# A running total of three propagation layers: its seven adds per layer move from VectorE to GpSimd

## The reference, cut to what matters

```
N_NODES = 18750; NNZ = 250000; LATENT = 64; MINI = 16; N_LAYERS = 3
def propagate(all_emb, rows, cols, vals):
    acc = all_emb
    x = all_emb
    for _ in range(N_LAYERS):
        x = segment_sum(vals[:, None] * x[cols], rows, num_segments=N_NODES)
        acc = acc + x
    return acc / (N_LAYERS + 1)
rating = sigmoid(users_emb @ items_emb.T + bias_user[users] + bias_item.T)
```

## Time and profile before

| what | us |
|---|---|
| median of 3 runs | 5368.86 |
| lowest and highest | 5368.59, 5371.43 |
| the profiled execution | 5364.2 |
| its span, first to last instruction | 5362.3 |
| VectorE busy | 4779.3 (89%) |
| TensorE matmul busy | 3360.9 (63%) |
| GpSimd busy | 2473.0 (46%) |
| ScalarE busy | 2466.3 (46%) |

### The profile page before, as it was taken

How to read it: one execution, slowest core, us unless ns; L and a number is a source line. 1 busy time by engine, 2 the same in 40 slices (tenths; PEclk the granted TensorE clock), 3 DMA queues, 4 the chain that set the end, 5 groups by cost and what they waited for, 6 DMA issues and landing times.

```text
span 5362.3 us, 195922 instructions
## 1 busy us (share of the span) xinstructions
PE 3360.9 (63%) x71235; PEld 2862.9 (53%) x71473; DVE 4779.3 (89%) x7551; ACT 2466.3 (46%) x4385; POOL 2473.0 (46%) x2179
## 2 busy tenths in 40 slices
PE   5600021111388888777688888867768888867767
PEld 4500011110377777666577777756657777766652
DVE  9989999999999999877899999967799999977778
ACT  0025555554466666500166666620046666640027
POOL 0038764433277777700067777720037777760000
PEclk9955555555699999999989999989989999989999
DMA  9960000300288877799978788889968877879999
GB/s 328 415 264 0 0 0 3 5 0 0 84 249 250 248 245 247 228 328 328 278 218 251 247 251 251 246 277 328 328 196 255 251 247 246 252 244 328 328 282 357
DMA packets 840271, 1191.20 MB, mean 222 GB/s; under 512 B 150791, under 2 KB 667582, under 8 KB 839824
## 3 DMA queue, kind: packets, MB, share of 16 engines
q1 hardware_dynamic: 716032, 816.66, 53.6%
q0 software_dynamic: 123872, 372.78, 18.2%
q10 hardware_dynamic: 304, 1.00, 0.1%
HBM read 638.35 MB, written 551.90 MB: 222 GB/s over the span
## 4 chain that ended last, share of the span: by engine, by line
DVE 27%; DMA 27%; issue 21%; POOL 10%; PE 7%; ACT 5%; SPq 1%; DVEq 1%; POOLq 0%; another core or an unknown queue 0%; ACTq 0%
DMA ring<-posts 15%; POOL posts L803 9%; DMA posts<-ring 8%; DVE store L1092 6%; PE psum L1543 4%; DVE total L889 3%; DVE ring L1313 3%; DVE store L1070 3%; ACT new L711 3%; DVE store L1071 2%; DMA out<-new 2%; DVE new L1285 2%; DVE ring L1337 2%; PE psum L1519 2%; DVE ring L1298 1%
## 5 line engine op out<-in xcount | busy, mean ns | idle before, releaser
L803 POOL DMA_INDIRECT posts<-ring x1884 | 1851.0, 982 | 1554.2 <-DVE ring L1298 962.3
L1519 PE MATMUL psum<-store,ring 128*128 x45216 | 2088.8, 197 | 485.0 <-DVE ring L1313 450.5
L1519 PEld LDWEIGHTS psum<-store,ring 128*128 128x128 bf16 x45216 | 1818.2, 100 | 755.7 <-issue 576.7
L711 ACT ACTIVATE new<-new 128x512 bf16<-128x512 uint8 x1884 | 1067.8, 614 | 0.0
L1313 DVE TENSOR_SCALAR ring<-ring,lane_f 128x1024 bf16<-128x1024 bf16 x1884 | 963.1, 553 | 10.7 <-DMA ring<-lanes_d 9.5
L1337 DVE TENSOR_TENSOR ring<-ring,wide_lane 128x1024 bf16<-128x1024 bf16 x948 | 613.3, 689 | 299.7 <-ACT ring L722 299.7
L1298 DVE TENSOR_TENSOR ring<-new 128x1024 bf16<-128x1024 bf16 x942 | 652.5, 693 | 92.4 <-ACT new L711 63.3
L709 ACT ACTIVATE ring<-new 128x512 bf16<-128x512 bf16 x942 | 585.8, 622 | 297.2 <-DVE new L1285 292.3
L767 POOL TENSOR_TENSOR ring<-store 128x1024 f32<-128x1024 f32 x157 | 369.6, 2354 | 662.7 <-DVE store L1010 306.4
L1285 DVE TENSOR_TENSOR new<-psum,vals_m 128x512 f32<-128x512 f32 x942 | 644.5, 684 | 6.9 <-PE psum L1519 4.9
L1429 PE MATMUL psum<-ident,store 128*128 128x128 f32 x224 | 51.6, 424 | 725.9 <-DVE store L1071 725.9
(11 more groups left out here) (232 smaller groups left out, 2728.0 us busy)
## 6 DMA issues: line engine op xcount, KB each, us to landing
ring<-lanes_d SPq DMA_DIRECT2D x471, 512.0 KB
ring<-posts SPq DMA_DIRECT2D x240, 772.0 KB, 6.7
store<-posts SPq DMA_DIRECT2D x234, 772.0 KB, 6.7
posts<-store SPq DMA_DIRECT2D x2, 30880.0 KB, 166.7
posts<-store SPq DMA_DIRECT2D x2, 30108.0 KB, 128.5
out<-new SPq DMA_DIRECT2D x96, 500.0 KB, 8.5
posts<-ring POOLq DMA_INDIRECT x1884
store<-L_rec_bias_item SPq DMA_DIRECT2D x1, 3125.0 KB, 14.6
```

What stands on the lines that cost most here:

```text
L711: last = nc.scalar.activation(digits[s][:, k, :], scaled_byte[s][k], ACT.Copy, scale=scale)
L803: pool.indirect_dma_start(out=posts[:, :], out_offset=bass.IndirectOffsetOnAxis(ap=dring[:, h, c:c + 1], axis=0), in_=msg[:, n, :], in_off ...
L1519: last = pe.matmul(psum[:, d % 4, (n % 2 * BLOCK + b) * F:(n % 2 * BLOCK + b + 1) * F], of, xflat[:, bass.ds(at_d[c] * F + (k * XT + x * F ...
```

## The change

GpSimd now runs the seven pieces of the running total at the head of each layer's program, ahead of its first scatter. In layer 0 it waits for the tables to be written (s_lanesd, s_decoded) and for x (s_x0), in the others for the last add of the layer before (s_add). VectorE's `take` and its seven calls are gone. The waits for s_taken stand as they were.

```
@@ gpsimd
             for layer in range(LAYERS):
                 done = layer * CHUNKS
+                if layer:
+                    pool.wait_ge(s_add, layer * ITERS + 2)
+                else:
+                    pool.wait_ge(s_lanesd, 64)
+                    pool.wait_ge(s_decoded, 1)
+                    pool.wait_ge(s_x0, 1)
+                for q in range(SPLITS):
+                    a, b = q * SPLIT, (q + 1) * SPLIT
+                    if layer == 0:
+                        nc.gpsimd.tensor_copy(total3[:, a:b, :], new3[:, a:b, :]).then_inc(s_taken, 1)
+                    else:
+                        nc.gpsimd.tensor_tensor(total3[:, a:b, :], total3[:, a:b, :], new3[:, a:b, :], ALU.add).then_inc(s_taken, 1)
+
                 def scatter(i, chunks):
@@ vector
-            def take(layer, q):
-                a, b = q * SPLIT, (q + 1) * SPLIT
-                if layer == 0:
-                    nc.vector.tensor_copy(total3[:, a:b, :], new3[:, a:b, :]).then_inc(s_taken, 1)
-                else:
-                    nc.vector.tensor_tensor(total3[:, a:b, :], total3[:, a:b, :], new3[:, a:b, :], ALU.add).then_inc(s_taken, 1)
-
@@ vector, send(i, first, pairs)
                         if not (first and d < 3):
                             low_parts(i, (d + 5) % 8, d - 3)
-                        if first and d < SPLITS:
-                            take(layer, d)
```

## The result

The changed kernel takes 5511.16 us in the median (3 runs, 5508.76 to 5518.41) against 5368.86: a ratio of 1.0264, interval 1.025 to 1.0278. It is slower, as forecast, but by 142 us and not by 31.5, far outside the range. Its profiled execution has a span of 5516.6, which is 154.3 above that of the kernel before.

What follows compares the result with a forecast made beforehand. VectorE was taken to bound the splits and first pairs. 24.6 us for layers 1 and 2 plus 6.9 for layer 0, gains deducted, made 31.5 on top of 5368.9: 5400.4 us, range 5376 to 5416.

Steps and rivals of the forecast that it cites:

- The split of layers 1 and 2: GpSimd's seven adds take turns with VectorE's 14 subtractions, making each of these splits 18.1 us longer.
- the first rival: In the splits, mixed-type subtractions don't exclude GpSimd; only the 13.7 us gain is left, 5355 us; chance 0.08.
- the second rival: GpSimd is kept out of the splits until the pairs begin, six adds delaying the first scatter; 5384 us; chance 0.08.
- the third: In the splits both engines share instead of excluding each other, at half the price; 5377 us; chance 0.06.
- Layer 0: GpSimd's seven copies, taken at 1.5 us each, make VectorE's chain ahead of the pairs 9.0 us later.
- the 0.9 won back: VectorE's own part in seven turns is 1.42 us in place of 1.55, 0.9 us less per layer.
- the lower bound of the earlier trace: Layer 0's copy at the memset's rate: 1.14 us for 1344 elements, VectorE's chain 6.5 us later.
- The gain in the first pairs: Pieces leaving VectorE bring pair 6 sooner: 2.1 us in layer 0, 5.8 each in layers 1 and 2, 13.7 in all.
- The stages are timed by each other, not by a clock, so an earlier start is kept: The first pairs' 13.7 us gain lasts to the end of each first half.
- If the split grows as foretold and the time still doesn't, the first half has a limit that I have not seen: Closing sign: longer splits without the foretold time would point to an unseen limit in the first half; no size given.

Runs made afterwards that it cites:

- x18: The changed kernel with one GpSimd add of one element behind layer 0's seven copies; 5377.51 us against 5344.68, ratio 1.0056.
- x8: The changed kernel with a one-element VectorE memset ahead of each pair's one-hot matrices; 5392.10 us, 43 above the kernel before.
- x5: The kernel before with one GpSimd copy of one element just before layer 0's first scatter; 5488.24 us, ratio 1.0212.
- x16: The kernel before with one GpSimd copy of one element and one add behind it, ahead of layer 0; 5342.68 us against 5342.72.
- x11: The kernel before with a one-element VectorE memset ahead of each pair's one-hot matrices; 5336.80 us, ratio 0.9986.

## Why the prediction was wrong, and where it was right

- **The split of layers 1 and 2: right.** Forecast 18.1 us each, measured 18.0. A turn of both engines is 4.29 us (2716.57 to 2725.16 is two), so GpSimd's own part is 2.87 beside VectorE's 1.42; the step had 2.9 and 1.42. Float32 and bfloat16 mixed exclude GpSimd as float32 alone does, which ends the first rival. The turn goes to and fro until the adds are done, 12 us before the one-hot matrices: not the second rival. All price and no sharing: not the third.
- **Layer 0: the copy was mis-sized, within its bounds.** Seven take 18.00 us in turns, 2.57 each; less VectorE's 1.42 that is 1.15 where the step took 1.5. 7 x 1.15 less the 0.9 won back is 7.1, and the split grew by 7.2 (forecast 9.0). It is the price of the memset, the lower bound of the earlier trace rows. The estimate from the Trainium skill's figure (GPSIMD Engine Reference, Elementwise — side-by-side cycle accounting) was 1.15 as well: the trace agrees.
- **The gain in the first pairs: right in size.** Forecast 2.1, 5.8 and 5.8. In the changed kernel it was 1.6, 5.4 and 4.8, and in x18, with scatters of the old length, 2.1, 6.4 and 6.3. The 25.6 us that the step took for pair 6 lie between the 25.0 and 26.8 of these. TensorE's granted clock in layer 1's first pairs (2758.2 to 2790) was 1.00, as the step had it, where it had been 0.61.
- **"The stages are timed by each other, not by a clock, so an earlier start is kept": the step that failed.** It asked only whether 13.7 us are kept, and took for granted that the pace of the other 307 pairs stays. They are timed by each other, and that makes them sensitive: a scatter 11 ns longer moved each one-hot matrix from just above to just below 91 ns behind a scatter. Two terms were put at nothing. Some 187 more scatters were held (201 against 14); at the 0.70 us of the rows above that is an estimate of 131 us. And 1884 scatters that are 11 ns longer are another 20. Of the 141 us that the scatters grew by from pair 6 on, that leaves 121 for the held turns, so the estimate is somewhat high; 19 us less between the scatters make it 122.
- **The order of GpSimd's instructions was in the text, and priced by its duration alone.** The views of before show the pace of the half, and no view shows that the kind of an earlier instruction matters. What could have been seen is the other link: the one-hot matrices of 1.09 us in place of 0.87 behind a scatter of 0.96, with starts 0.10 apart. That is a turn decided by little, in a loop of 942 rounds, and a line in the rivals with 100 us against it would have widened the range.
- **"If the split grows as foretold and the time still doesn't, the first half has a limit that I have not seen"** is what came true. With that limit taken away, x18 has the forecast's sum: 32.8 us measured (22 to 37 by its interval), 31.5 foretold. That the two are so close is partly luck: x18's splits and first pairs, read from its trace, add up to 43.2 - 14.8 = 28.4.

What stays open: why a copy as the last computing instruction ahead of layer 0's scatters makes each of the 1884, and the gathers behind the layers (most often 952 ns in place of 944), about 10 ns longer, and not those ahead of it, and why a copy ahead of layer 1 does nothing. The runs show the rule for this program, not what inside GpSimd is behind it. And the step from 11 ns to the edge is argued from the rows; that the lost turns are most of the cost is shown by x8, and that the 11 ns by themselves are some 20 us of it is an estimate.

## What to carry to other kernels

A stage in which two engines take turns in every round can have a pace that hangs on which of them comes first, here by some ten nanoseconds. Look there for the shortest distance between their starts and for an instruction that takes longer by a fixed amount, and price the case that the turn falls the other way, whatever the edit. When a stage that the edit doesn't touch becomes slower, compare the undisturbed duration of its most frequent instruction before looking for lost overlap, and try the new instructions at the size of one element: here that found nearly the whole loss in one run.

## What the runs showed of the hardware

- In these two kernels a one-hot matrix (bfloat16, one large input in SBUF) that starts 92 ns or more behind the start of a scatter lets it finish, and VectorE waits in the second instruction of the two; at 91 or less the scatter is nearly always held, though it began first. The kernel before had 589 of the first kind and 4 of the second at 92 or more, the changed one 188 held and 7 kept at 91 or less. Between 92 and 99 the changed kernel has 13 held beside 37 kept, so the edge is not sharp, and it is not the same in every kernel: with a memset ahead of the one-hot matrices (x8) 63 were kept and 3 held at 82 to 91.
- A GpSimd copy of 0.18 us, 75 us ahead of the first scatter, costs 138.7 us (x5), and an add of 0.20 us behind it takes that back (x16).
- GpSimd's and VectorE's two-input instructions exclude each other with mixed types too: 4.18 to 4.38 us in place of 1.55. A GpSimd copy of 1344 float32 takes part in the turns as an add does, at 1.15 us of its own beside 2.87.
- A memset of one element on VectorE in each pair made the kernel before 0.14% faster (x11).
